# x loaded two tiles at a time, a later load of the fourth context pair, and a K restack in two parts

## What is computed

```python
q = _split_heads(queries @ Wq)          # queries: layernorm(x); 16 heads of 16
k = _split_heads(keys @ Wk)             # keys, values: ctx_1024
v = _split_heads(values @ Wv)
scores = jnp.einsum('bhqd,bhkd->bhqk', q, k)
attn = jax.nn.softmax(scores, axis=-1)
out = jnp.einsum('bhqk,bhkd->bhqd', attn, v)
out = out.transpose(0, 2, 1, 3).reshape(queries.shape[0], queries.shape[1], D)
return out @ Wo
...
x = x + _L0_xattn_ref(_layernorm(x, axis=-1), ctx_1024, ctx_1024, mask_B_ik0, ...)
x = x + _L0_attn_ref(_layernorm(x, axis=-1), L0_attn_wq, L0_attn_wk, L0_attn_wv, L0_attn_wo)
x = x + _L0_ffn_ref(_layernorm(x, axis=-1), L0_ffn_W_in, L0_ffn_b_in, L0_ffn_W_out, L0_ffn_b_out)
```

## Time and profile before

| | |
|---|---|
| median of 3 executions | 637.76 us (636.15 to 639.42) |
| the profiled execution | 638.59 us, of which 636.8 us from the first to the last instruction |
| TensorE busy | 591.1 us (93%) |
| DVE, ACT, POOL busy | 464.2 (73%), 377.1 (59%), 190.2 us (30%) |
| mean granted TensorE clock | 0.983 of full speed |

### The profile page before, as it was taken

The page is one execution under the profiler, slowest core; times in us unless marked ns, Lnnn a source line. Parts: engine busy times, 40 slices in busy tenths (PEclk is TensorE's granted clock), DMA queues, the critical chain, the costliest instruction groups (busy, mean ns, idle before and its releaser), DMA issues. The chain is left out here.

```text
span 636.8 us, 17469 instructions
## 1 busy us (share of the span) xinstructions
PE 591.1 (93%) x6765; PEld 514.9 (81%) x6770; DVE 464.2 (73%) x977; ACT 377.1 (59%) x1011; POOL 190.2 (30%) x243
## 2 busy tenths in 40 slices
PE   6689999999999899997798999999999999899897
PEld 3578888898889788996687888888989898644597
DVE  4557788888878778875899756565666656678797
ACT  3567788888878788873322424343433333558884
POOL 6522233333333333672411212121212111260400
PEclk9789999999999999999899999999999999999999
DMA  6995767777768768840400000000000000000012
GB/s 205 259 245 147 196 150 192 161 204 158 209 149 205 162 166 220 209 154 1 134 2 11 3 3 1 3 1 2 3 3 1 2 3 2 2 0 2 0 50 83
DMA packets 37073, 58.93 MB, mean 93 GB/s; under 512 B 6913, under 2 KB 15233, under 8 KB 36993
## 3 DMA queue, kind: packets, MB, share of 16 engines
q1 hardware_dynamic: 29328, 42.75, 26.7%
q10 hardware_dynamic: 4592, 8.78, 4.9%
q0 software_dynamic: 3072, 6.30, 4.2%
HBM read 17.96 MB, written 2.10 MB: 31 GB/s over the span
## 5 line engine op out<-in xcount | busy, mean ns | idle before, releaser
L704 ACT ACTIVATE Pr<-pS,nmax 128x256 f32<-128x256 f32 x256 | 120.0, 483 | 27.0 <-DVE nmax L818 25.9
L818 DVE TENSOR_REDUCE nmax<-pS 128x2 f32<-128x512 f32 x128 | 87.4, 683 | 23.5 <-PE pS L542 22.2
L1045 POOL TENSOR_TENSOR a_Pr<-a_Pr,a_rinv 128x512 f32<-128x512 f32 x32 | 32.7, 1044 | 182.9 <-DVE a_rinv L1327 182.9
L552 PE MATMUL pT<-ident,Pr 128*128 128x128 f32 x512 | 78.9, 277 | 2.7 <-DVE wraw L823 2.4
L542 PE MATMUL pS<-Kst,Qst 96*128 96x256 f32 x256 | 59.1, 314 | 14.4 <-ACT Pr L704 5.5
L1213 ACT ACTIVATE a_Pr<-a_Pr 128x512 f32<-128x512 f32 x32 | 20.2, 631 | 78.9 <-DVE a_Pr L1319 78.9
L552 PEld LDWEIGHTS pT<-ident,Pr 128*128 128x128 f32 x512 | 60.4, 143 | 3.9 <-issue 3.9
L542 PEld LDWEIGHTS pS<-Kst,Qst 96*128 96x128 f32 x256 | 40.8, 196 | 22.7 <-issue 12.1
L704 ACT ACTIVATION_READ_ACCUMULATOR Pr<-pS,nmax 128x1 f32 x256 | 54.8, 214 | 0.0
L324 POOL DMA_DIRECT2D Qst<-QSh x60 | 30.3, 508 | 75.1 <-PE pS L542 71.4
L59 PE MATMUL a_pJ<-Kst,XTh 128*128 128x512 f32 x64 | 27.9, 437 | 3.0 <-ACT a_V L1208 3.0
(11 more groups left out here) (365 smaller groups left out, 2079.6 us busy)
## 6 DMA issues: line engine op xcount, KB each, us to landing
Kst<-WO_ints SPq DMA_DIRECT2D x96, 128.0 KB, 3.3
CT<-ctxT ACTq DMA_DIRECT2D x16, 512.0 KB, 5.0
Kst<-KSh SPq DMA_DIRECT2D x62, 128.0 KB, 3.1
Qst<-QSh POOLq DMA_DIRECT2D x64, 64.0 KB, 3.1
Qst<-QSh SPq DMA_DIRECT2D x64, 64.0 KB, 2.8
Kst<-KSl SPq DMA_DIRECT2D x31, 128.0 KB, 3.3
Qst<-QSl POOLq DMA_DIRECT2D x32, 64.0 KB, 2.8
Qst<-QSl SPq DMA_DIRECT2D x32, 64.0 KB, 2.7
```

Of the source, the lines that this page charges most:

```text
L552: last = pe.transpose(pT[s % 2][:, t, k, :], Pr[s % 2][:, t, P * k:P * k + P], ident[:, :])
L704: act.activation(Pr[c % 2][:, t, :], pS[c % 2][:, t, :], ACT.Exp, bias=nmax[c % 2][:, t:t + 1], accum_out=rsum[par][:, c // 4, 2 * (c % 4) ...
L818: dve.tensor_reduce(nmax[s % 2][:, :], pS[s % 2][:, :, :], AX.X, ALU.max, negate=True).then_inc(maxed, 1)
L1045: pool.tensor_tensor(rows, rows, rinv[s][:, :].unsqueeze(2).to_broadcast([P, 8, SQ]), ALU.mult).then_inc(weighted, 1)
```

## The change

SP's program: x is loaded in eight transfers of one quad each, and each has a semaphore of its own. Quads 0 and 1 come where tiles 0 to 3 came; quads 2 and 3 come behind the restack of pair 1's K; quads 4 to 7 come one each at the head of loop bodies 0 to 3. The restack of pair 1's K is started in two parts: group 0 ahead of the restack of pair 1's Q, and groups 1 to 3 behind it. ACT's program: the load of context pair 3 moves from ahead of the loop to step 2 of quad 0. DVE's program: it waits for quad i + 2 ahead of `statistics` at step 4 in each body up to the sixth, and not at step 12 of the first.

```diff
-            load_x(0, 2, x_in0)
+            load_x(0)
             for m in W_ORDER[1:]:
                 load_w(m)
-            load_x(2, 2, x_rest[0])
+            load_x(1)
...
             restack_first_q(sp, qst_sync[0], (0, 1))
+            restack_k(sp, 1, 7, 0, (0,))
             restack_q(sp, qst_sync[1], 1, 3, 0, (0, 1))
-            load_x(4, 4, x_rest[1])
-            restack_k(sp, 1, 7, 0)
-            load_x(8, 8, x_rest[2])
+            restack_k(sp, 1, 7, 0, (1, 2, 3))
+            load_x(2)
+            load_x(3)
 
             def body(i, last):
                 late = isinstance(i, int) and i == QUADS - 2
                 if not last:
+                    if i + 4 < QUADS:
+                        load_x(i + 4)
                     restack_k(sp, 0, EV0 + EV * i + 2, CHUNKS * (2 * i + 1))
...
-            load_ctx(3, 1, 2)
             exps(0, 0)
...
+                    if s == 2 and first:
+                        load_ctx(3, 1, 2)
...
-                    if s == 4 and first:
-                        dve.wait_ge(x_rest[1], 16)
-                    if s == 12 and first:
-                        dve.wait_ge(x_rest[2], 16)
+                    if s == 4 and two_ahead(i):
+                        dve.wait_ge(x_in[i + 2], 16)
                     if s == 4 and i + 2 <= QUADS:
                         statistics(i, i + 2)
```

More of the change, by code:

```diff
@@ L252, in cross_attention @@
         pY = ps("pY", [P, D])
-        x_in0, x_rest = sem("x_in0"), [sem(f"x_rest{n}") for n in range(3)]
+        x_in = [sem(f"x_in{n}") for n in range(QUADS)]
         w_in = [sem(f"w_in{m}") for m in range(4)]
@@ L369, in _, with load_x @@
         def _(sp):
[L370 to L373, removed]
+            def load_x(quad):
+                sp.dma_start(X[:, 2 * quad:2 * quad + 2, :],
+                             x[2 * P * quad:2 * P * quad + 2 * P, :].rearrange("(t p) d -> p t d", p=P)
+                             ).then_inc(x_in[quad], 16)
             def load_w(m):
@@ L864, in _ @@
             dve.tensor_tensor(CS[0][LO][:, :, :], CT[0][:, :, :], f32(CS[0][HI][:, :, :]), ALU.subtract).then_inc(ctx_lo, 1)
-            dve.wait_ge(x_in0, 16)
+            dve.wait_ge(x_in[0], 16)
             statistics(0, 0)
@@ L876, in _ @@
                     split_w(3)
-                    dve.wait_ge(x_rest[0], 16)
+                    dve.wait_ge(x_in[1], 16)
                     statistics(0, 1)
```

## The result

The changed kernel takes 641.49 us (median of 20 executions, 638.63 to 643.50), the kernel before 636.75 (20 executions, 633.87 to 639.42). The ratio is **1.0076, 95% interval 1.0062 to 1.0090**: slower by some 4.8 us. The forecast was 639.3, slower by 1.5 and in the band of no change; the measured time lies within its range, near the upper end and next to the rival in which the contexts go first (642.2). By the prediction's own limit, 640.9, the kernel is slower, which had a chance of 0.19.

The account below looks back on a forecast made before the run. The prediction took start-up transfers to bound the change, TensorE's wait at step 8 mattering most. +1.7 us for quad 2's late landing less 0.2 for the clock gave +1.5, from 637.76 to 639.3 us; range 635.6 to 642.3.

Parts of the forecast that it names:

- the band of no change: Whole kernel: a time from 634.6 to 640.9 us, about 0.5% or 3.2 us either way; chance 0.72.
- SP's chain: SP's queue at start-up: last K of pair 1 issued by 36.2, 1.5 us later than before; quad 2's load follows.
- The landing of quad 2: Load of quad 2, issued at 36.2: lands at 42.0, between bounds of 38.3 and 44.7.
- the engines do not run dry meanwhile: DMA engines from 25.6 to 30.3: POOL's Q, K and SP's Q give 5.5 us of work.
- Rival 3: Start-up: context pairs 3 and 4 go ahead of quad 2, landing 44.7, +4.4 us, 642.2; chance 0.16.
- The quick landing: Quad 2's load: 2.6 us by the skill page's estimate, landing at 38.8, which speaks for the early bound.
- From the landing to TensorE: Step 8: TensorE released 2.7 us after quad 2 lands, at 44.7 against 42.98 before, +1.7 us.
- The clock: Falls in TensorE's wait before step 8, as before; up to 0.8 us given back, taken as 0.2.
- What waits no longer: Step 8: pair 1's K restack lands at about 41, holds nobody; its 3.0 us TensorE wait is gone.
- The base: The kernel before: profiled execution 638.59 us, 0.83 above the median 637.76 to which the change was added.
- The rest near nothing: Later context pair 3, four more SP issues, pair 2's K restack and DVE's piled-up work: each taken as 0.

Follow-up runs that it names:

- the last run: The kernel before with only the loads of context pairs 3 and 4 moved to steps 5 and 7 of quad 0: ratio 0.9983, 634.95 us.

## Why the prediction was right, and where it was short

The direction was right, and so was the path: SP comes late to quad 2, DVE waits for it, and TensorE waits for what DVE does next. The run with the statistics at step 7 shows it. The size was a third of the measured one, 1.5 against 4.8 us, and one term did that. By its steps:

- **SP's chain.** Forecast 36.2 for the load of quad 2, measured 36.38, and 36.7 in the second profile. The split cost what the issue times said.
- **The landing of quad 2.** This is the term that was mis-sized. I took 5.9 us, for a landing at 42.0; it took 8.3 (44.7) and 6.9 (43.6). The bytes were about right, both contexts among them: the engines moved 258 GB/s x 20.9 us = 5.39 MB from 22 us to K's landing before, and 223 x 22.7 = 5.06 MB from 22 us to quad 2's landing now, 0.33 MB fewer where my count had 0.26. The step that failed is "the engines do not run dry meanwhile". They did, with a share of 0.43 from 29 to 32 us against 1.09 before. I had laid POOL's 384 KB of Q between 25.6 and 30.3, but POOL issued them from 22.2 to 24.7 and they had landed by 29.0, and SP's Q came at 64 KB per 0.62 us. At 258 GB/s the 5.06 MB would have been moved by 41.6, near the forecast; at 223, and 230 in the second profile, they were not.
- **Rival 3.** Its landing, 44.7, and its time, 642.2, came close, with a chance of 0.16. Its mechanism, that the two contexts are served ahead of quad 2, is not shown as the reason: my count had them ahead as well. With one context less behind 32 us the landing took 4.9 us, but then the gap was smaller too, and no run separates the two. The later context took part in either case: with the split it made the gap deeper, and it came when K and quad 2 were due.
- **The quick landing.** The 2.6 us that I estimated from the Trainium skill, DMA: Bandwidth & Descriptors, section Anatomy of one DMA — SWDGE (gpsimd) path, did not come near either. Its fit is for transfers that GpSimd issues, and SP issues these.
- **From the landing to TensorE.** Forecast 2.7, measured 47.54 - 44.68 = 2.86, and 2.85 in the second profile.
- **The clock.** It fell and came back at 53.0, 5.5 us after TensorE resumed, against 5.9 before. Little was given back, as taken.
- **What waits no longer.** The K restack landed at 35.7 + 7.9 = 43.6, not near 41, and it held nobody, as said. That TensorE's wait came out at 4.75 us, within the 4 to 5 expected, is luck: both of its ends were late, `weigh` by 2.8 us (42.78 against 39.97), and in the second profile the wait was 6.2.
- **The base.** I set the change against a profile of 638.59 us with a second wait of 3.0 us and a stretch at low clock behind it. The second profile, 633.33, has neither. The wait at step 8 was there in both profiles of the changed kernel. Also, the median of my three executions, 637.76, was 1.0 us above that of the 20, 636.75.
- **The rest near nothing.** Pair 2's K restack began at 47.03 and was not waited for. The context alone was neutral (0.9994), as predicted; beside the late quad 2 it likely was not (1.0076 against 1.0055). The first wait was longer in the profile after, and that is not the change's doing.

The landing and the base account for the difference. With 44.7 for 42.0 the forecast would have been 2.7 us higher, 642.0, against 641.49 measured. The 0.6 that then lack to 4.8 are less than the 1.0 us by which I had the base too high.

## What to carry to other kernels

A load that is put later for the sake of others must be followed to its reader, and past it: here the reader was DVE, in program order ahead of the row maximum on which the whole loop hung, and moving the wait by three steps took back most of the loss without moving a byte. When transfers set the time, count not only their bytes but whether the engines stay busy: here the list of transfers stood still behind one that was not ready, and went on with small ones, and the DMA share fell to 0.43. Idle time earlier on (10 to 13 us here) and work that nobody needs soon (two contexts) are the things to use; each edit measured 0.9983, both together 0.9946. And a wait that ends on a transfer may be absent from the next execution: take a second profile before it goes into a sum.

## What was unexpected of the hardware

The first wait, for pair 0's Q, came in two kinds in 14 profiles: 3.8 to 4.9 us in nine of them, 5.4 to 5.8 in five (the changed kernel, two made from it, the first with quad 2 at the start, and the last run, made from the kernel before). It goes with the first projection of all, at 8 us. Before, second profile of before, and the kernel with statistics at step 7:

```profile
8.04 0.58 PE L59 MATMUL pJ<-CS0h,Wh 128*128 128x512 f32 x1
```
```profile
7.94 0.47 PE L60 MATMUL pJ<-CS0h,Wh 128*128 128x512 f32 x1
```
```profile
8.17 0.99 PE L59 MATMUL pJ<-CS0h,Wh 128*128 128x512 f32 x1
```

In the nine that matmul took 0.47 to 0.58 us, in the five 0.82 to 0.99, where the same shape takes 0.39 a little later. So TensorE ran slow for longer at the start in the five, and their first K and Q restacks began 0.4 to 1.2 us later than the mean of the nine. The granted clock reads 1.00 at 8 us in both kinds (before, and statistics at step 7), so the profile does not say what was slow. The waits differ by more than that. Why a small delay grows was not tried; an explanation that was only argued is that the last Q transfers then come to stand behind the context that ACT starts near 20 us. One of the five is an execution of a kernel whose order up to there is that of before but for context pair 3, and the changed kernel fell in both kinds, so the kernel alone does not decide it. All five do load context pair 3 late, as do four of the nine. That load stands behind 20 us, so it cannot come before the slow matmul at 8 us; with 14 profiles it may be chance.

The clock also came back at different times in executions of one kernel: at 31.8 and 34.3 us in the two profiles of before, at 36.0 and 31.9 in those of the changed kernel. With this and the first wait the end of `weigh` lies anywhere from 40.0 to 42.8 us in these four, and so does the start of any wait behind it.
